# A linear layer in tiles of 64 rows, in a kernel of convolutions and adapted linear layers

## The reference

```python
x = x + _L0_ffn_ref(_L0_cond_ref(x, ...), ...)   # low-rank part folded into W
x = x + _L1_ffn_ref(_L1_cond_ref(x, ...), ...)   # top-2 of 8 experts of rank 16
x = x + _L2_ffn_ref(_L2_cond_ref(x, ...), ...)   # a low-rank pair per batch of 16 samples
x = x + _L3_ffn_ref(_L3_cond_ref(x, ...), ...)   # top-1 of 4 experts of rank 8
```

## Time and profile before

| what | value |
|---|---|
| median of three runs | 1254.17 us |
| the profiled execution's own time | 1256.99 us |
| its span, first to last instruction | 1255.1 us |
| TensorE busy | 1203.0 us, 96% |
| DVE, ACT, POOL busy | 514.4, 357.7, 543.1 us |
| mean granted TensorE clock | 0.989 |

### The profile page before, as it was taken

One profiled execution on the slowest core, in us unless ns is written; L12 is line 12 of the kernel. 1 busy time (PEld: TensorE's weight loads), 2 busy tenths in 40 slices (PEclk: granted clock), 3 DMA queues, 4 the chain that ended last, 5 costly groups with the idle time before them and its releaser, 6 DMA issues.

```text
span 1255.1 us, 46113 instructions
## 1 busy us (share of the span) xinstructions
PE 1203.0 (96%) x21528; PEld 692.1 (55%) x21528; DVE 514.4 (41%) x986; ACT 357.7 (28%) x762; POOL 543.1 (43%) x411
## 2 busy tenths in 40 slices
PE   5799899999999999999999999999999999999997
PEld 3345555655555556655556556555565545565555
DVE  6932334343444343433344334344334333434343
ACT  2332233133322222223222223223222222313321
POOL 4636436444235555344355551555343434644400
PEclk9888999999999999999999999999999999999999
DMA  6333200001423000002122100002101200000101
GB/s 202 135 121 142 103 2 2 2 30 33 170 69 137 3 3 2 2 3 95 69 69 71 67 3 2 2 2 95 69 36 66 73 3 2 2 2 26 46 4 66
DMA packets 21453, 63.72 MB, mean 51 GB/s; under 512 B 4528, under 2 KB 5296, under 8 KB 17040
## 3 DMA queue, kind: packets, MB, share of 16 engines
q1 hardware_dynamic: 19344, 59.27, 13.1%
q10 hardware_dynamic: 1920, 1.52, 0.4%
HBM read 42.95 MB, written 17.83 MB: 48 GB/s over the span
## 4 chain that ended last, share of the span: by engine, by line
PE 87%; DVE 3%; issue 2%; DMA 0%; ACT 0%; DVEq 0%
PE bank_b L1298 27%; PE bank_a L117 13%; PE bank_a L104 11%; PE bank_b L104 11%; PE bank_b L87 8%; PE bank_a L1235 5%; PE bank_a L75 3%; PE bank_b L1256 3%; PE bank_b L1250 2%; PE bank_b L1310 2%; PE bank_b L1291 1%; DVE z L1141 1%; PE bank_b L1269 1%; PE bank_b L1279 1%; PE bank_b L1312 1%
## 5 line engine op out<-in xcount | busy, mean ns | idle before, releaser
L907 POOL TENSOR_TENSOR sum_v<-raw_v 128x768 f32<-128x768 f32 x30 | 55.4, 1847 | 592.7 <-ACT raw_v L965 592.7
L1298 PE MATMUL bank_b<-w_hi,y3t_hi 128*128 128x512 f32 x512 | 208.8, 408 | 1.5 <-issue 1.5
L1298 PE MATMUL bank_b<-w_lo,y3t_hi 128*128 128x512 f32 x512 | 202.7, 396 | 2.9 <-issue 2.9
L1298 PE MATMUL bank_b<-w_hi,y3t_lo 128*128 128x512 f32 x512 | 203.1, 397 | 0.3 <-issue 0.3
L117 PE MATMUL bank_a<-y,w_down 64*32 64x512 f32 x3072 | 172.2, 590 | 0.0
L104 PE MATMUL bank_b<-y,wv 32*64 32x512 f32 (+2 forms) x3584 | 146.2, 486 | 5.8 <-ACT y L327 5.8
L104 PE MATMUL bank_a<-y,wv 32*64 32x512 f32 (+2 forms) x3584 | 145.2, 484 | 3.7 <-issue 3.7
L1091 DVE TENSOR_TENSOR x<-bank_b,x 128x512 f32<-128x512 f32 x96 | 66.4, 692 | 197.9 <-PE bank_b L1298 159.1
L959 ACT ACTIVATE y<-bank_a,cb,tab 128x512 f32<-128x512 f32 x64 | 49.6, 777 | 316.9 <-PE bank_a L117 311.8
L1298 PEld LDWEIGHTS bank_b<-w_hi,y3t_hi 128*128 128x128 f32 x512 | 96.9, 189 | 36.7 <-issue 15.5
L87 PE MATMUL bank_b<-xs,cw 32*32 32x512 f32 x3072 | 111.4, 609 | 0.4 <-PEq L232 0.4
(11 more groups left out here) (194 smaller groups left out, 1493.0 us busy)
## 6 DMA issues: line engine op xcount, KB each, us to landing
w_hi<-w_scratch SPq DMA_DIRECT2D x9, 1024.0 KB, 5.0
w_lo<-w_scratch SPq DMA_DIRECT2D x9, 1024.0 KB, 8.3
x_in<-in_x SPq DMA_DIRECT2D x32, 256.0 KB, 4.3
out_x<-out_tile SPq DMA_DIRECT2D x32, 256.0 KB, 2.4
w_raw<-in_w SPq DMA_DIRECT2D x3, 1024.0 KB, 10.5
w_scratch<-w_hi SPq DMA_DIRECT2D x3, 1024.0 KB, 4.5
w_scratch<-w_lo SPq DMA_DIRECT2D x3, 1024.0 KB, 6.9
w_raw<-w_scratch SPq DMA_DIRECT2D x2, 1024.0 KB, 9.9
```

The lines of the kernel that those rows point to most:

```text
L907: ins = g_.tensor_tensor(dst[:, :, at:at + count].rearrange("p r k o -> p r (k o)"), src[:, :, 0:count].rearrange("p r k o -> p r (k o)"), ...
L1298: ins = pe.matmul(lin_ps[b][:], y3t[yi][:, k, P * b:P * (b + 1)], w[use(m) % 2][wi][:, k], start=(k == 0 and i == 0), stop=(k == KB - 1 an ...
```

## The change

The linear layer's matmuls take 64 rows each, half of a block of 128 contracted values. base(m, pair, swap) works on two quarters of the tokens at a time: with swap 0 the upper 64 rows go to the first quarter's bank and the lower 64 to the second's, with swap 1 the other way round. So two matmuls that follow each other use different rows of the array and different banks. After both swaps each bank has its whole sum. The semaphore half_done separates the two swaps of a pair.

The order around them changes too. In layers 1 and 3 TensorE does base(0, swap 0), to_tokens, products, base(0, swap 1), adapter_turn, base(1, 0), adapted 0 and 1, base(1, 1), adapted 2 and 3. As the second pair's banks are now written at the same time, z's transposes go to bank_a[3], and TensorE waits before them until ACT has copied the products. In layers 0 and 2 without "effective" it does base(0, 0), base(1, 0), products, base(0, 1), base(1, 1). With "effective" it does base(0, 0), effective, products, base(0, 1), the wait for w_sum_ready, base(1, 0), base(1, 1), effective. DVE's residuals in layers 0 and 2 wait for both quarters of a pair.

```diff
-    zt_ps = logit_ps
+    zt_ps = bank_a[3]
...
-                dve.wait_ge(lin_done, tiles(m, b + 1))
+                dve.wait_ge(lin_done, tiles(m, b + 1 if l in (1, 3) else b // 2 * 2 + 2))
...
                 pe.wait_ge(z_ready, before(m, (1, 3)) + 1)
+
+                if m + 2 < PHASES:
+                    pe.wait_ge(raw_ready, tiles(m + 2, ROWS))
+                    pe.wait_ge(ghosts_ready, tiles(m + 2, ROWS))
...
-            def base(m, b):
-                l = layer(m)
+            def base(m, pair, swap):
+
+
+                HALF = P // 2
+                last = swap == 1 and layer(m) in (0, 2)
+                if swap:
+
+                    pe.wait_ge(half_done, ROWS * m + 2 * (pair + 1))
                 for k in range(KB):
                     for i, (yi, wi) in enumerate(PASSES):
-                        ins = pe.matmul(lin_ps[b][:], y3t[yi][:, k, P * b:P * (b + 1)], w[use(m) % 2][wi][:, k],
-                                        start=(k == 0 and i == 0), stop=(k == KB - 1 and i == 2 and l in (0, 2)))
-                if l in (0, 2):
-                    ins.then_inc(lin_done, 1)
+                        for h in range(2):
+                            b, rows = 2 * pair + (h + swap) % 2, slice(HALF * h, HALF * (h + 1))
+                            ins = pe.matmul(lin_ps[b][:], y3t[yi][rows, k, P * b:P * (b + 1)],
+                                            w[use(m) % 2][wi][rows, k], start=(swap == 0 and k == 0 and i == 0),
+                                            stop=(last and k == KB - 1 and i == 2), skip_group_check=True)
+                            if not swap and k == KB - 1 and i == 2:
+                                ins.then_inc(half_done, 1)
+                            if last and k == KB - 1 and i == 2:
+                                ins.then_inc(lin_done, 1)
...
             def linear_back(m):
+                base(m, 0, 1)
                 adapter_turn(m)
-                base(m, 2)
+                base(m, 1, 0)
                 pe.wait_ge(zt_ready, before(m, (1, 3)) + 1)
-                for b in range(3):
+                for b in range(2):
                     adapted(m, b)
-                base(m, 3)
-                adapted(m, 3)
+                base(m, 1, 1)
+                for b in (2, 3):
+                    adapted(m, b)
...
-                base(m, 0)
+                base(m, 0, 0)
                 effective(m, 0)
                 if adapts:
                     to_tokens(m)
-                    base(m, 1)
+                elif m % STEP not in EFF:
+                    base(m, 1, 0)
                 if n + 1 < PHASES:
                     products(n + 1)
                 if adapts:
                     linear_back(m)
                 else:
-                    base(m, 1)
+                    base(m, 0, 1)
                     if m % STEP in EFF:
                         pe.wait_ge(w_sum_ready, summed(m) + 2)
-                    base(m, 2)
-                    base(m, 3)
+                        base(m, 1, 0)
+                    base(m, 1, 1)
                     effective(m, 1)
```

More of the change, by code:

```diff
@@ L745, in main_program @@
     xs_ready, xb_ready, c2_done, dn_done = (keep[n] for n in ("xs_ready", "xb_ready", "c2_done", "dn_done"))
-    tr_done = sem("tr_done")
+    tr_done, half_done = sem("tr_done"), sem("half_done")
     c0_done, pr_done, w2s_ready, v_sums, wv_ready, raw_ready, ghosts_ready, y0_act, y0_dve = (
@@ L1309, in adapted @@
                     for i, (zi, bi) in enumerate(PASSES):
-                        ins = pe.matmul(lin_ps[b][:], zt[zi][:, tokens], keep["b1"][bi][:], start=False, stop=(i == 2))
+                        ins = pe.matmul(lin_ps[b][:], zt[zi][:, tokens], keep["b1"][bi][:], start=False, stop=(i == 2),
+                                        skip_group_check=True)
                 else:
                     ins = pe.matmul(lin_ps[b][:], zt[0][0:len(PASSES) * E3 * R3, tokens], keep["b3s"][:],
-                                    start=False, stop=True)
+                                    start=False, stop=True, skip_group_check=True)
                 ins.then_inc(lin_done, 1)
```

## The result

The changed kernel took 1334.68 us (median of four runs, 1334.37 to 1338.43), 1.0641 times the kernel before, 95% interval 1.062 to 1.0662. With one more run, the kernel before has a median of 1255.37 us in this comparison. Slower was forecast, and it is slower, but by 79 us instead of 45: 1334.7 lies above the range that ended at 1322.

What follows compares the result with a forecast made beforehand. TensorE was taken as the bound, 87% of the chain that ended last. Terms 0 + 20 + 3 + 18 + 2.6 + 1.2 gave +45 us on 1256.99, so 1302, less 2.8 to the median: 1299, range 1262 to 1322.

Steps and rivals of the forecast that it cites:

- The pace, 0 for 1536 pairs: Linear layer's base matmuls: a pair of 64-row halves takes 0.2325 us, like one whole matmul; change 0.
- A: Rival on base matmuls: alternating halves hide what each has beyond streaming, pair 0.216 us, total 1274; chance 0.18.
- C: Rival on base matmuls: loads and streams collide, pair 0.240 to 0.245, 1311 to 1318, or 1464; chance 0.12.
- D: Rival on base matmuls: the fp32r halves run one after the other, +357 us, total 1656; chance 0.05.
- E: Rival for the whole kernel, faster than 1248 us, outside the range; chance 0.03; its reason is cut from the text.
- Changes of tile size, +20 and +3: TensorE switching between 64-row and whole-array blocks: +20 us in layers 1 and 3, +3 us in "effective" phases.
- rival B: Switching between 64 x 128 and 128 x 128 tiles drains nothing: -23 us, total 1276; chance 0.12.
- Instructions, +1.2: TensorE's issue waits: 3072 more instructions on 43056, 7% of 17.4 us of waits, +1.2 us.
- The wait for w_sum, +18: Before base(1, 0) in "effective" phases, TensorE waits for DVE's late effective adds: 2.24 us x 8, +18 us.
- half_done, +2.6: Between base(1, 0) and base(1, 1) in "effective" phases: wait for the last matmul, 0.32 us x 8, +2.6 us.
- the cover of z: Layer 1's second transposes: TensorE's existing 0.54 us wait for z hides added changes of 0.06 + 0.14, -1.6 us.
- Edits at nothing: Waits for ACT's copies, late residuals with POOL's scaled input, and DMAs: all covered or unmoved, no cost.

Runs made afterwards that it cites:

- experiment 5: Changed kernel in its 64-row tiles, three things mended: POOL's sums wait for z, effective banks added first, products earlier in plain phases; 1274.82 us, ratio 1.0148.
- whole rows: Changed kernel with the same three things mended as in experiment 5, but base blocks of 12 matmuls of 128 rows; 1256.96 us, ratio 1.0016.
- experiment 1: Changed kernel, but POOL's sums of the products wait in layer 1 until z is ready; 1296.87 us, ratio 1.0327.
- experiment 4: Kernel before, in whole 128-row matmuls, with only the products moved ahead of base 1 in layer 1; 1287.91 us, ratio 1.0238.

## Why the prediction was right or wrong

- **The pace, 0 for 1536 pairs: right.** 0.2327 us for a pair of 64 rows, 0.2325 for a matmul of 128, so the height of the tile made no difference here, and rivals A, C, D and E (the side faster than 1248) fell. No run of the kernel before shows the pace of a pair: 0.2325 for it was the author's estimate, and the runs showed 0.2327. Nor does any run show that a matmul has something beyond streaming, which A supposes. Its 0.216 was an estimate too, half of the 0.43 between fp32 matmuls (0.434), and it was seen in neither shape.
- **Changes of tile size, +20 and +3: right in size.** Each change costs what was read from another pair of sizes, 0.09 + 0.11, and rival B fell. With half_done the forecast was 1.14 us in a phase of layer 1, 1.34 in layer 3 and 0.72 in an "effective" phase; measured are 1.16, 1.31 and 0.72, in all 25.5 for 25.6.
- **Instructions, +1.2: the wrong sign.** The waits for issue did not grow with 3072 more instructions. They fell from 17.4 to 11.2 us in the changed kernel, and are 12.9 in the mended tiles against 17.2 in whole rows. That is why the mended pair shows 17.9 for all that the tiles bring, where 27 had been forecast.
- **The wait for w_sum, +18: right, but without the clock.** From 595.04 TensorE's next pair came at 597.44, 2.40 us instead of 0.23, and the one after it 0.11 late: 2.28 in all, where 2.24 had been forecast, in eight phases. Undoing it gave 22.3. What was wrong is the sentence "The clock should hold", argued from one stretch with 1.1 us of idling. In three of the eight it didn't: the granted clock was 0.50 behind them.
- **half_done, +2.6: right**, 0.37 for 0.32.
- **The step that failed** is that the cover of z was taken to be unchanged: "In the 8 phases of layer 1 TensorE already waits 0.54 us for z", with only TensorE's own delays set against it, and "DMAs and their queues are unmoved" as all that was asked of the other engines. The products were moved ahead of a base block. Their cost on TensorE is the same there, so no term was written for the move. But they release ACT's copies and then POOL's sums, which now start 2.7 us earlier, within DVE's gating instead of behind it. Experiments 1 and 4 show it from both sides: 37.8 us back when POOL waits, 31.2 lost when only the products move. Of the 37.8, 24.3 is the wait; the other 13.5 goes with the clock, which no longer halved behind it and halved less often behind w_sum.
- **Edits at nothing.** ACT's copies into bank_a were hidden, as said. POOL's scaled input was argued for the end of the residuals only. In plain phases the products now come later, and POOL's sums, which stand ahead of the scaled input on its queue, pushed that past the down tiles: the 4.7 us of waiting for xs. With the products earlier (experiment 5) this wait is gone.

So the account of the 79 us by experiments: 37.8 for POOL against DVE with the clock, 22.3 for DVE's order with the clock, 17.9 for the tiles, 0.6 for the rest, 78.6 together. That the parts add up rests on one measurement: undoing the first two together left 1274.8, where 1274.6 follows from undoing each alone.

The two traces give the same by another way, as an estimate. Tiles 25.5, w_sum 8 x 2.28 = 18, z 26.0 - 4.3 = 22, xs 5, issue -8 (11.2 instead of 19.1, with one more wait of 1.7 before), and the clock. It was 0.975 over 1336.0 us and 0.989 over 1255.1, that is 33 and 14 us short of full speed, so 19 more. Together 81 to 82, and the spans differ by 80.9. Put so, the forecast's own terms stand at 25.5 + 18 instead of 25.6 + 18, and what it lacked is z, 22, and the clock, 19.

## What to carry to other kernels

When a block is moved in one engine's program, ask what its result releases, and lay the released work over every other engine's critical stretch: a move that is neutral on its own engine cost here 37.8 us, more than the tiles themselves. Where short DVE instructions with two inputs in SBUF stand on a critical chain, look at what POOL does on SBUF beside them: two of 0.19 us took 1.86 and 1.68 here; one wait on POOL, the engine with slack, bought all of it back. And here, where whole matmuls already hid their weight loads (0.19 us each, in steps of 0.2325), tiles of half the rows gained nothing (0.2327 for a pair), and each change of tile size into an fp32r block cost 0.2 us.

## What the runs showed of the hardware that had not been expected

- A DVE instruction of 0.19 us with two SBUF inputs took 1.86 beside a POOL sum that had started 0.03 us earlier; it ended 0.05 us after that sum, and was back at 0.19 when POOL waited (experiment 1). Instructions with one SBUF input beside the same sums kept 0.18 and 0.19.
- A wait of 3.5 us in an otherwise full TensorE cost about 1.5 us again in the clock, granted at 0.50 for 3.3 us: 4.5 us for a block of 3.0. In the changed kernel it happened behind all eight waits for z (2.4 to 3.5 us) and three of the eight of 2.0 for w_sum. It doesn't always: in experiment 4 two of six waits of 3.5 us were followed by a granted clock of 1.00, and in experiment 1 seven of the eight of 2.0.
